# Shorter lags between the steps of the expert tiles in a fused attention and mixture-of-experts layer (one Trainium2 core)

## The reference

```python
shared = einsum('bls,ds->bld', silu(einsum('bld,sd->bls', x, sfc1)) * einsum('bld,sd->bls', x, sfc2), sfc3)
top_w, top_idx = top_k(einsum('bld,ed->ble', x, gate_w), 2)      # softmax over the two
h = silu(einsum('td,ehd->teh', xf, w1))                          # D=256 -> H=128 per expert
moe = einsum('teh,te,edh->td', h, dispatch, w2)                  # dispatch: the two weights
x = x + layernorm(moe + shared)
```

## Time and profile before

| | us |
|---|---|
| device time, median of 3 runs | 903.46 |
| lowest and highest of them | 901.47, 910.64 |
| span of the profiled execution | 941.9 |
| TensorE busy | 789.9 (84%) |
| VectorE busy | 652.5 (69%) |
| ScalarE busy | 519.9 (55%) |
| GpSimd busy | 370.8 (39%) |

### The profile page before, as it was taken

One profiled execution on the slowest core, in us unless ns is written; L12 is line 12 of the kernel. 1 busy time (PEld: TensorE's weight loads), 2 busy tenths in 40 slices (PEclk: granted clock), 3 DMA queues, 4 the chain that ended last, 5 costly groups with the idle time before them and its releaser, 6 DMA issues. The chain is left out here.

```text
span 941.9 us, 14973 instructions
## 1 busy us (share of the span) xinstructions
PE 789.9 (84%) x4690; PEld 491.1 (52%) x4690; DVE 652.5 (69%) x1256; ACT 519.9 (55%) x1047; POOL 370.8 (39%) x442
## 2 busy tenths in 40 slices
PE   4688998999989989899688779899978877778884
PEld 3433343443434434334233358777757777777773
DVE  4488689797887988967679457777644444443785
ACT  1226577776777767767567633344324554545363
POOL 4430171631715417144100104566650555556342
PEclk9869799998999999989989989999999888988997
DMA  7856528737578275672664013453545344445994
GB/s 153 236 119 179 123 62 203 158 105 168 91 179 177 92 178 96 151 175 88 151 113 181 1 48 108 141 179 120 169 157 176 113 143 131 134 140 184 268 180 90
DMA packets 112421, 133.29 MB, mean 142 GB/s; under 512 B 16724, under 2 KB 80726, under 8 KB 112344
## 3 DMA queue, kind: packets, MB, share of 16 engines
q1 hardware_dynamic: 98616, 108.39, 45.9%
q0 software_dynamic: 13248, 23.15, 9.4%
q10 hardware_dynamic: 480, 0.79, 0.5%
HBM read 68.18 MB, written 59.87 MB: 136 GB/s over the span
## 5 line engine op out<-in xcount | busy, mean ns | idle before, releaser
L480 DVE TENSOR_REDUCE negmax<-ring 128x2 f32<-128x1024 f32 x256 | 307.0, 1212 | 85.1 <-PE ring L643 84.0
L430 ACT ACTIVATE probs<-scores 128x512 f32<-128x512 f32 x498 | 273.6, 599 | 110.8 <-PE scores L661 107.7
L661 PE MATMUL scores<-q_st,k_st 64*128 64x512 f32 x498 | 207.5, 475 | 30.2 <-ACT probs L430 15.1
L643 PE MATMUL ring<-k_st,q_st 48*128 48x512 f32 x512 | 185.6, 480 | 22.5 <-DMA k_st<-rows_in 7.2
L661 PEld LDWEIGHTS scores<-q_st,k_st 64*128 64x128 f32 x498 | 83.7, 192 | 178.3 <-ACT probs L430 108.4
L675 PE MATMUL av<-probs,v_aug 128*32 128x512 f32 x1024 | 142.5, 630 | 6.3 <-ACT probs L430 6.3
L331 POOL CAST part_r<-negmax 128x16 fp32r<-128x16 f32 x32 | 7.6, 237 | 210.0 <-DVE negmax L480 210.0
L643 PEld LDWEIGHTS ring<-k_st,q_st 48*128 48x128 f32 x512 | 72.6, 198 | 33.3 <-issue 20.4
L1534 POOL DMA_INDIRECT rows_out<-m_y,projected x48 | 47.3, 985 | 66.0 <-ACT m_y L1599 53.2
L166 POOL TENSOR_TENSOR scratch<-qk_raw,cos 128x512 f32<-128x512 f32 x29 | 37.1, 1278 | 79.5 <-ACT qk_raw L383 78.4
L1685 DVE TENSOR_TENSOR m_h_lo<-scores,m_h_hi 128x512 fp32r<-128x512 f32 x40 | 27.7, 692 | 53.7 <-ACT m_h_hi L1585 42.9
(11 more groups left out here) (253 smaller groups left out, 1672.2 us busy)
## 6 DMA issues: line engine op xcount, KB each, us to landing
q_st<-rows_in SPq DMA_DIRECT2D x96, 128.0 KB, 4.6
k_st<-rows_in SPq DMA_DIRECT2D x90, 128.0 KB, 5.5
experts<-split SPq DMA_DIRECT2D x8, 1024.0 KB
projected<-records SPq DMA_DIRECT2D x48, 129.0 KB
split<-O SPq DMA_DIRECT2D x24, 256.0 KB, 2.8
experts<-rows_out SPq DMA_DIRECT2D x10, 512.0 KB, 9.8
m_rows<-records SPq DMA_DIRECT2D x32, 129.0 KB, 2.1
X<-in_x SPq DMA_DIRECT2D x8, 512.0 KB, 5.0
```

Source lines behind the costliest of these rows:

```text
L430: nc.scalar.activation(probs[r // 2 % 2][r % 2][:, a, :], score_of(R)[:, a, :], ACT.Exp, scale=HD ** -0.5).then_inc(exp_done, 1)
L480: nc.vector.tensor_reduce(negmax[Gn % 2][:, t, 2 * p:2 * p + 2], ring[t % 2][:, :, :], AX.X, ALU.max, negate=True).then_inc(max_done, 1)
L643: last = nc.tensor.matmul(half[:, a, :], q[rows, t * P:(t + 1) * P], k[rows, :], start=True, stop=True)
L661: nc.tensor.matmul(score_of(R)[:, a, :], k[rows, kt * P:(kt + 1) * P], q[rows, :], start=True, stop=True).then_inc(sc_ps, 1)
```

## The change

The lags are shortened. T goes two steps ahead of F where it was one, and stands behind F inside the step. silu runs in the same step as its pair's F and red. G follows one step behind F where it was two, O one step behind where it was three, scale two steps behind where it was four, and scale is first in ScalarE's step where it was last; x_hi is last where it was first. The number of instructions, their sizes, the waits' meanings and the order of SyncE's and GpSimd's work stay.

Inside step s after the change:

- TensorE: G(s-1), F(s), T(s+2), O(s-1)
- ScalarE: scale(s-2), g_hi(s-1), silu(s), x_hi(s+2)
- VectorE: x_lo(s+1), g_lo(s-1), red(s)

```diff
-        X_AHEAD, SILU_LAG, TURN_LAG, OUT_LAG = 1, 1, 2, 3
-        STEPS = range(-X_AHEAD, PAIRS + OUT_LAG + 1)
+        X_AHEAD, TURN_LAG, OUT_LAG, SCALE_LAG = 2, 1, 1, 2
+        STEPS = range(-X_AHEAD, PAIRS + SCALE_LAG)
...
             for s in STEPS:                                      # ScalarE
-                x, i, t, o = s + X_AHEAD, s - SILU_LAG, s - TURN_LAG, s - OUT_LAG - 1
-                if of(x):
-                    act.wait_ge(xt_s, x + 1)
-                    if x > 1:
-                        act.wait_ge(mh_s, x - 1)
-                    nc.scalar.copy(x_hi[x % 2], bank_x[x % 2]).then_inc(xhi_s, 1)
+                x, i, t, o = s + X_AHEAD, s, s - TURN_LAG, s - SCALE_LAG
+                if of(o):
+                    act.wait_ge(my_s, o + 1)
+                    if o >= HELD:
+                        act.wait_ge(sent[(o - HELD) % LOADS], 32 * ((o - HELD) // LOADS + 1))
+                    for f in range(2):
+                        nc.scalar.activation(y[o % HELD][:, f, :], bank_o[o % 2][:, f, :], ACT.Copy,
+                                             scale=rows[o % LOADS][:, f, D:D + 1]).then_inc(scaled_s, 1)
                 if of(t):
...
                 if of(i):
                     act.wait_ge(pre_s, i + 1)
                     nc.scalar.activation(g[i % 2][:, :, :], g[i % 2][:, :, :], ACT.Silu).then_inc(msilu_s, 1)
-                if of(o):
...
+                if of(x):
+                    act.wait_ge(xt_s, x + 1)
+                    if x > 1:
+                        act.wait_ge(mh_s, x - 1)
+                    nc.scalar.copy(x_hi[x % 2], bank_x[x % 2]).then_inc(xhi_s, 1)
...
             for s in STEPS:                                      # VectorE
-                x, t = s + X_AHEAD, s - TURN_LAG
+                x, t = s + X_AHEAD - 1, s - TURN_LAG
...
             for s in STEPS:                                      # TensorE
-                if of(x):
-                    pe.wait_ge(loaded[x % LOADS], 32 * (x // LOADS + 1))
-                    if x > 1:
-                        pe.wait_ge(xlo_s, x - 1)
-                    ...
                 if of(t):
...
                     last.then_inc(mh_s, 1)
+                if of(x):
+                    pe.wait_ge(loaded[x % LOADS], 32 * (x // LOADS + 1))
+                    if x > 1:
+                        pe.wait_ge(xlo_s, x - 1)
+                    for f in range(2):
+                        for c in range(DC):
+                            last = nc.tensor.transpose(bank_x[x % 2][:, f, c, :], rows[x % LOADS][:, f, c * P:(c + 1) * P], ident[:, :])
+                    last.then_inc(xt_s, 1)
```

## The result

Before, 20 timed runs beside the changed kernel have a median of 907.65 us (897.98 to 914.21); after, 20 runs have 915.11 us (906.53 to 921.54). The ratio is 1.0089, with a 95% interval of 1.0065 to 1.0114: slower by 0.9%, or 7.5 us, at the edge of what the forecast called no change (1%). The ratio leaves out the slowest executions, which had a lower granted clock (of after 921.54 us at 0.937 and 921.48 at 0.944); the medians have them all. The forecast was 921 us and a rise of 17.5 us. The direction is right, the rise is less than half of it. The forecast counted from 903.46, the median of three runs; the 20 runs have 907.65, so of the 10 us by which the rise fell short 4.2 are this base and 5.9 the level after.

What follows compares the result with a forecast made beforehand. The prediction took GpSimd's scatters (2.58 us per pair) to bound the kernel before, and a closed queue path of 2.97 us the changed one. Shared expert start at 843.6 plus 77.5 gave 921.1 us; range 902 to 933.

Steps and rivals of the forecast that it cites:

- The ring: Tiles: closed queue path silu, x_hi, scale, g_hi, g_lo, red, silu on ScalarE and VectorE; 2.97 us per pair.
- Start: Start of the tiles: first scatter at 727.4 instead of 731.43, 4.0 us earlier.
- Register loads: TensorE's sequencer loads 16 registers at five of the steps; 5 x 0.24 = 1.2 us added.
- End: After the last pair: shared expert starts at 843.6, behind t_hi and t_lo; the rest takes 77.5 us.
- The level: Whole changed kernel: the forecast's summed time, 843.6 + 77.5 = 921.1 us.
- the scatters bound the tiles: Kernel before, timed runs: GpSimd's scatters set 2.58 us per pair; the profile's gaps belong to the profiled execution.
- The shorter way of a pair also frees the nine row buffers sooner; that is worth nothing: Row buffers in the tiles: no gain, since loads don't set the pace at 2.58 or 2.97 us per pair.
- the sum for before: Whole kernel before: last scatter at 834.3 instead of 870.8, 36.5 us less, giving 905.4 us.
- Rival A: Tiles: GpSimd stays the bound at 2.58 us per pair; end 904.6 us, no change; chance 0.20.
- Rival B: Tiles: gaps are real in timed runs too, from a shortage of row buffers; 879.5 us, faster; chance 0.10.
- Rival C: TensorE's clock: 26% of pairs meet the slow level at 1.35 us more each; 935 us; chance 0.15.
- The span stays near 940: Profile after: if gaps come from the amount of records per pair, a pair costs 3.67 us before and after.

Runs made afterwards that it cites:

- Experiment 2: Kernel after with g_hi(s-1) ahead of scale(s-2) in ScalarE's step; 903.75 us, ratio to before 0.9936.
- experiment 3: Kernel after with red(s) ahead of g_lo(s-1) in VectorE's step; 935.84 us, ratio 1.0274.
- 4: Kernel after with scale last in ScalarE's step, behind silu and x_hi; 914.34 us, ratio 1.0078.
- 9: Kernel after with silu, G, O and scale one step later each and g_hi ahead of scale, timed again; 897.21 us, ratio 0.9897.
- Experiment 1: Kernel before, profiled once more with no edit; 911.49 us, span 909.7.
- experiments 5 to 7: Row buffers, nine originally: kernel before with eight, 929.72 us; kernel after with eight, 917.28 us; kernel before with ten and three y buffers, 900.74 us.

## Why the prediction was right, and where it was not

**The ring (2.97 us per pair): shown.** Each step is in the timelines, the sum is 2.98. Experiment 2 took one link out and the pace fell to 2.66; 3 closed another ring, through TensorE; 4 left the circle as it was and the pace too; 9 opened it.

**Start.** The first scatter comes 11.03 us after the first T; forecast 727.4 - 719 = 8.4. The granted clock was 0.72 of full there, where the rows of the forecast had 1.00. Before again, it is 13.88. So the gain was 2.85 us, forecast 4.0. This is one profile of each kernel.

**Register loads.** Forecast 5 x 0.24 = 1.2 us, measured 4 x 0.75 = 3.0. The 0.62 us of the earlier trace rows were listed as a wait for rows, so how much of them was the load could not be read there.

**End.** T to the last scatter's end: forecast 847.8 - 719.0 = 128.8, measured 839.1 - 707.1 = 131.9. First T to the shared expert's first product: forecast 124.6, measured 128.6 (835.75). As forecast it follows t_lo, 834.41 + 1.29 = 835.70. The rest took 911.0 - 835.75 = 75.3, forecast 77.5. From first T to the end that is 203.9 against 202.1.

**The level.** 921.1 becomes 915.1 thus: the first T stands 11.9 earlier than in the profile of before (719.04; in the eleven other profiles it lies between 706.4 and 715.5); the sum from T on is 1.8 longer; an execution is 1.8 longer than its span (912.8 and 911.0); and the median is 2.3 above this execution. 921.1 - 11.9 + 1.8 + 1.8 + 2.3 = 915.1. The nearness of the two numbers owes something to luck: errors that cancel.

**The step that failed** is the one on before: "in a timed run the scatters bound the tiles", and with it "The shorter way of a pair also frees the nine row buffers sooner; that is worth nothing". It took all 36.5 us of gaps out and left before a stage of 834.3 - 719.0 = 115.3 us. Experiment 1 has 125.4: 8.6 us of gaps, for which experiments 5 to 7 show the cause, too few row buffers (with a share of the clock in two of the nine gaps, experiment 1), and 1.5 us in the start. From first T to the end, before takes 909.7 - 711.5 = 198.2, not 905.4 - 719.0 = 186.4: the sum for before was 11.8 us short, the one for after 1.8. The change closed the ring, at (2.98 - 2.58) x 39 = 15.6 us and 3.0 for the register loads; it gave back the 8.6 us of waits for rows and 2.85 of the start. 15.6 + 3.0 - 8.6 - 2.85 = 7.2; the stage grew by 131.9 - 125.4 = 6.5, the medians by 7.5. The terms come from one profile of each kernel, and such an account is not exact to 1 us.

**Rival A** (GpSimd stays the bound, 2.58) fell: 2.98, and 40 waits of GpSimd. **Rival B** (the gaps are real, from a shortage of buffers) named the right mechanism and was mis-sized: 8.6 us, not 38. Its argument against, that T at 735.36 had its rows and its result still came late, holds for that execution alone. I weighed B as all or nothing, and the right case was a part of each. **Rival C** (the clock) fell: over the 120.9 us of tiles the granted clock was 1.00 with TensorE busy 109.09, idle 0.3 us a step in pieces. The Trainium skill ("TensorE: Matmul & The Clock Gate", section "A second HAM failure mode: psum-queue depth-cycling") tells of another kernel whose frequent short idle times made the clock swing. In these 39 steps the trace does not show that.

**"The span stays near 940"** was wrong: 911.0. It rested on the gaps coming from the amount of records. After has the same work per pair, and no profile taken later has such gaps, whichever kernel it is of. The Trainium skill ("NOTIFIC — the notification-queue block", section 7.1) says that the block holds producers back rather than lose a record inside it. That this made the pauses each 11 us was a reading of the prediction. With the same 14973 instructions in the profile that has the pauses and in those of experiment 1 and of after, which don't, nothing is left that speaks for it here. What stopped that one execution stays open.

## What to carry to other kernels

Shorter lags between in-order engines pay only until a path closes that runs once around two queues: list the queues, follow one item from an instruction back to itself through what stands ahead of it, add up the starts, and compare the sum with the bound of the stage; the order within a step counts as a circle. A lag also has a price in the time for which buffers are held, here 16.2 us from T to the end of scaling before the change and 12.0 after, so a shortage shows up as small waits for loads well away from the engine that is the bound. If the profiled span is far above the timed runs (here 941.9 against 903.46), take a second profile before judging which of its waits are real.

## What the runs showed that was not expected

- One profiled execution of twelve had some 28 us of pauses that no instruction explains: T's record ended at 735.96, and the x_hi released by it began at 740.21. In the second profile of before T ends at 767.60 + 0.66 = 768.26 and x_hi begins at 768.29.
- Where TensorE's sequencer loads 16 registers, a closed ring turns 0.75 us later (after) or 1.4 us later (experiment 3), depending on whether TensorE is in the ring.
- The number of row buffers mattered as much as the change or more: 929.7, 907.9 and 900.7 us with 8, 9 and 10 in the kernel before (with 10, one `y` buffer fewer).
